# GpSimd multiplies rows and edges, and ScalarE takes half of the exponentials tile by tile, in the slots behind the last transfer of a graph-attention pass

## The reference, cut to what matters

```python
e = jax.nn.leaky_relu(feat_src[src] + feat_dst[dst]); e = jnp.sum(e * attn, axis=-1)
ee = jnp.exp(e - segment_max(e)[dst])
alpha = ee / segment_sum(ee)[dst]                 # one share per edge and head
msg = softmax(en * r_feat * alpha, axis=-1)       # en = feat_src[src], over the 32 features
g_agg = segment_sum(msg, dst)
```

## Time and profile before

| what | value |
|---|---|
| median of three runs | 5961.28 us |
| the profiled execution | 5973.71 us, span 5971.6 us |
| the tail from the end of the long loop to the final projection | about 5705 to 5914 us of the span |
| of it, steps after the last softmax piece | about 5758.7 to 5900.8 us |

### The profile page before, as it was taken

The page is one execution under the profiler, slowest core; times in us unless marked ns, Lnnn a source line. Parts: engine busy times, 40 slices in busy tenths (PEclk is TensorE's granted clock), DMA queues, the critical chain, the costliest instruction groups (busy, mean ns, idle before and its releaser), DMA issues. The chain is left out here.

```text
span 5971.6 us, 92359 instructions
## 1 busy us (share of the span) xinstructions
PE 4194.8 (70%) x31126; PEld 3201.6 (54%) x31126; DVE 2727.6 (46%) x6953; ACT 2238.6 (37%) x5687; POOL 3172.5 (53%) x3030
## 2 busy tenths in 40 slices
PE   4777777777867777778757577676666676666656
PEld 2444444444445555544557566566565665566646
DVE  6635444444211111234322355655556556466586
ACT  2555555555300000156200045445454454444520
POOL 4645545555145555553066566565555655565645
PEclk9898888888667777888555567676677766667776
DMA  2323343343257777400122223333333333333332
GB/s 83 144 99 141 141 155 150 149 155 147 91 208 256 255 251 257 153 9 7 46 53 51 59 70 85 79 85 85 76 84 79 79 89 74 80 86 81 85 84 64
DMA packets 324619, 660.29 MB, mean 111 GB/s; under 512 B 124556, under 2 KB 208454, under 8 KB 316232
## 3 DMA queue, kind: packets, MB, share of 16 engines
q1 hardware_dynamic: 230246, 581.33, 27.6%
q0 software_dynamic: 92160, 74.67, 7.7%
q10 hardware_dynamic: 1896, 0.12, 0.0%
HBM read 393.69 MB, written 262.14 MB: 110 GB/s over the span
## 5 line engine op out<-in xcount | busy, mean ns | idle before, releaser
L1667 POOL DMA_INDIRECT gath<-fs_scratch,src_idx x1568 | 1615.4, 1030 | 1158.1 <-issue 459.9
L681 POOL DMA_INDIRECT gath<-in_x,src_idx x720 | 767.4, 1066 | 724.9 <-PE sum_x_ps_g L791 442.1
L1716 PE MATMUL ps_e<-fdw,scratch 128*128 128x66 f32 x3136 | 789.7, 337 | 395.8 <-issue 195.1
L729 ACT ACTIVATE scratch<-sum_x_ps_c 128x800 bf16<-128x800 f32 x932 | 763.0, 836 | 669.6 <-PE sum_x_ps_c L748 469.0
L1796 ACT ACTIVATE scratch<-scratch,bias,weight 128x32 f32<-128x32 f32 x2608 | 931.2, 403 | 55.1 <-DVE bias L1869 47.8
L1718 PE MATMUL ps_e<-gath,ident 128*128 128x66 f32 x3136 | 785.8, 336 | 151.4 <-issue 150.7
L681 POOL DMA_INDIRECT gath<-y_scratch,src_idx x592 | 597.2, 1009 | 543.1 <-PE sum_y_ps_g L791 353.2
L1716 PEld LDWEIGHTS ps_e<-fdw,scratch 128*128 128x128 f32 x3136 | 639.6, 249 | 454.5 <-issue 419.2
L1779 ACT ACTIVATE scratch<-ps_o 128x512 f32<-128x512 f32 x394 | 227.9, 596 | 1446.9 <-remote 844.8
L748 PE MATMUL sum_x_ps_c<-e_tab,scratch 128*128 128x400 bf16 x1864 | 541.2, 378 | 320.1 <-ACT scratch L729 171.2
L1718 PEld LDWEIGHTS ps_e<-gath,ident 128*128 128x128 f32 x3136 | 648.3, 252 | 161.6 <-issue 161.4
(11 more groups left out here) (276 smaller groups left out, 5308.2 us busy)
## 6 DMA issues: line engine op xcount, KB each, us to landing
count_scratch<-scratch SPq DMA_DIRECT2D x60, 3200.0 KB
scratch<-count_scratch SPq DMA_DIRECT2D x240, 800.0 KB
en_scratch<-gath SPq DMA_DIRECT2D x196, 264.0 KB
scratch<-en_scratch SPq DMA_DIRECT2D x196, 264.0 KB
scratch<-in_edge_attr_2x SPq DMA_DIRECT2D x390, 128.0 KB
gath<-fs_scratch,src_idx POOLq DMA_INDIRECT x1568
fdw<-fd_scratch SPq DMA_DIRECT2D x392, 33.0 KB
gath<-in_x,src_idx POOLq DMA_INDIRECT x720
```

The costliest lines, as they stand in the source:

```text
L681: pool.indirect_dma_start(out=gath[:, s, t, 0:F], out_offset=None, in_=table_dram, in_offset=bass.IndirectOffsetOnAxis(ap=src_idx[:, g, k: ...
L729: act.activation(counts[:, b % 2, :, unit["column"]:unit["column"] + 2 * q] .rearrange("p a (h d) -> p h a d", h=2), ps_c[u % 2][:, :, 0:q ...
L1667: pool.indirect_dma_start(out=gath[:, s, t, :], out_offset=None, in_=fs_dram, in_offset=bass.IndirectOffsetOnAxis(ap=src_idx[:, g, k:k + 1 ...
L1716: pe.matmul(ps_e[g][:, k, 0:ROW], oht[:, s % 2, g * K + k, :], fdw[:, s, g, :], start=True, stop=False)
```

## The change

In the tail, the product of rows and edges moves from DVE to POOL. POOL makes it for slot n + 1 at the head of step n, ahead of its other work for slots n and n - 1; the product of the first tail slot is made before the tail begins. DVE waits for it (`tail_multiplied`) before it takes the maximum. The slot is then divided: tiles 0 to 3 go the way of the long loop (DVE copies the shares into `weight`, makes `bias` = - maximum x share, and ACT makes eight small exponentials with scale, bias and `accum_out`), tiles 4 to 7 the way of the tail before (POOL takes off the maximum and multiplies by the shares, ACT makes one exponential over the half). DVE sums only tiles 4 to 7. The long loop is unchanged.

```diff
+                def multiply(n, q):
+                    pool.wait_ge(loaded[q], arrived(n, q))
+                    feats = en[:, q, :, 0:HID]
+                    pool.tensor_tensor(feats, feats, r[:, q, :, :], ALU.mult).then_inc(tail_multiplied, 1)
 
                 def step(m, n, q, piece):
+                    if exists(n, -1):
+                        multiply(n + 1, (q + 1) % SLOTS)
                     if exists(n, 0):
                         pool.wait_ge(top_ready, n + 1)
-                        pool.tensor_tensor(heads(q), heads(q), each(bias[:, q, :]), ALU.subtract).then_inc(centred, 1)
+                        pool.tensor_tensor(later(q), later(q), of_later(bias[:, q, K * H:]), ALU.subtract)\
+                            .then_inc(centred, 1)
                         pool.wait_ge(centred, n - (TAIL - 1))
-                        pool.tensor_tensor(heads(q), heads(q),
-                                           each(a_tab[:, bass.ds(n * SG, SG), :, :].rearrange("p g k h -> p (g k h)")),
+                        pool.tensor_tensor(later(q), later(q),
+                                           of_later(a_tab[:, bass.ds(n * SG + 1, 1), :, :]
+                                                    .rearrange("p g k h -> p (g k h)")),
                                            ALU.mult).then_inc(scaled, 1)
...
+                multiply(TAIL, TAIL % SLOTS)
                 tail(pool, lambda it: None, step)
...
-                        if m is None:
-
-                            act.wait_ge(scaled, n - (TAIL - 1))
-                            act.activation(en[:, q, :, 0:HID], en[:, q, :, 0:HID], ACT.Exp).then_inc(exp_done, 1)
-                        else:
-                            act.wait_ge(bias_ready, n + 1)
-                        for i in range(ST * H if m is not None else 0):
+                        act.wait_ge(bias_ready, n + 1)
+                        for i in range(ST * H if m is not None else K * H):
...
+                        else:
+                            act.wait_ge(scaled, n - (TAIL - 1))
+                            act.activation(en[:, q, K:, 0:HID], en[:, q, K:, 0:HID], ACT.Exp).then_inc(exp_done, 1)
...
-                    if exists(n, 0):
+                    if exists(n, 0) and m is not None:
                         dve.wait_ge(loaded[q], arrived(n, q))
                         feats = en[:, q, :, 0:HID]
                         dve.tensor_tensor(feats, feats, r[:, q, :, :], ALU.mult).then_inc(multiplied, 1)
...
+                    if exists(n, 0) and m is None:
+                        shares = a_tab[:, bass.ds(n * SG, 1), :, :].rearrange("p g k h -> p (g k h)")
+                        dve.tensor_copy(weight[:, q, 0:K * H], shares)
+                        dve.wait_ge(top_ready, n + 1)
+                        dve.scalar_tensor_tensor(bias[:, q, 0:K * H], bias[:, q, 0:K * H], -1.0, shares,
+                                                 ALU.mult, ALU.mult).then_inc(bias_ready, 1)
...
-                        first = K if m is not None else 0
                         dve.wait_ge(exp_done, n)
-                        dve.tensor_reduce(total[:, q1, first * H:], en[:, q1, first:, 0:HID]
+                        dve.tensor_reduce(total[:, q1, K * H:], en[:, q1, K:, 0:HID]
```

More of the change, by code:

```diff
@@ L1523, in build, with arrived @@
                                 "msg_ready", "oh_msg_ready", "summed", "added"))
-            centred, scaled = sem("centred"), sem("scaled")
+            centred, scaled, tail_multiplied = sem("centred"), sem("scaled"), sem("tail_multiplied")
             block = ctx.enter_context(nc.Block())
             r_view = edge_attr.rearrange("e h f -> e (h f)")
+            def arrived(n, q):
+                if not isinstance(n, int):
+                    return slot_count(n, q, 16 * (1 + SG))
+                count = 0
+                for i in range(q, n + 1, SLOTS):
+                    count += 16
+                    for g in range(SG):
+                        count += 16 * (E - (i * SG + g) * GROUP >= K)
+                return count
             def walk(engine, before, step, lag=LAG):
@@ L1677, in each, with later, of_later @@
                     return wide(columns.rearrange("p (t h) -> p t h", h=H), 3, [P, ST, H, F])
+                def later(q):
+                    return en[:, q, K:, 0:HID].rearrange("p t (h f) -> p t h f", h=H)
+                def of_later(columns):
+                    return wide(columns.rearrange("p (t h) -> p t h", h=H), 3, [P, ST - K, H, F])
+                def multiply(n, q):
+                    pool.wait_ge(loaded[q], arrived(n, q))
+                    feats = en[:, q, :, 0:HID]
+                    pool.tensor_tensor(feats, feats, r[:, q, :, :], ALU.mult).then_inc(tail_multiplied, 1)
                 def step(m, n, q, piece):
+                    if exists(n, -1):
+                        multiply(n + 1, (q + 1) % SLOTS)
                     if exists(n, 0):
                         pool.wait_ge(top_ready, n + 1)
-                        pool.tensor_tensor(heads(q), heads(q), each(bias[:, q, :]), ALU.subtract).then_inc(centred, 1)
+                        pool.tensor_tensor(later(q), later(q), of_later(bias[:, q, K * H:]), ALU.subtract)\
+                            .then_inc(centred, 1)
                         pool.wait_ge(centred, n - (TAIL - 1))
-                        pool.tensor_tensor(heads(q), heads(q),
-                                           each(a_tab[:, bass.ds(n * SG, SG), :, :].rearrange("p g k h -> p (g k h)")),
+                        pool.tensor_tensor(later(q), later(q),
+                                           of_later(a_tab[:, bass.ds(n * SG + 1, 1), :, :]
+                                                    .rearrange("p g k h -> p (g k h)")),
                                            ALU.mult).then_inc(scaled, 1)
@@ L1859, in step @@
                     if exists(n, 0):
-                        dve.wait_ge(multiplied, n + 1)
+                        if m is not None:
+                            dve.wait_ge(multiplied, n + 1)
+                        else:
+                            dve.wait_ge(tail_multiplied, n - (TAIL - 1))
                         dve.tensor_reduce(top[:, :] if m is not None else bias[:, q, :],
@@ L1921, in step @@
                                           ALU.mult).then_inc(msg_ready, 1)
[L1923 to L1932, removed]
                 def row(n, lo=0, hi=P):
```

## The result

The changed kernel took 6000.82 us (median of 20 runs, 5951.84 to 6032.07) against 5964.05 us before (20 runs, 5915.14 to 6000.28): ratio 1.0056, 95% interval 1.0036 to 1.0077, so it is 21 to 46 us slower. The forecast was +25 us with T = 5.86 us a step, and "same" within 1%. The direction and the mechanism held; the size was on the low side. "Same" alone tells little: by the prediction's own sums it would have held for every T up to 7.05, so the tail has to tell the cases apart.

What follows compares the result with a forecast made beforehand. POOL with its port to DVE bounds the tail's step, the four-slot ring nearly tight; +27.8 us from a two-step round and -2.7 from softmax steps make +25, 5986 us, range 5946 to 6014.

Steps and rivals of the forecast that it cites:

- T: Time per message step in the tail's repeating part, 29 steps: 4.90 us before, forecast 5.86, adding 27.8 us.
- The round over two steps: Tail's slot ring, messages j to messages j + 2, closes over two steps instead of three: 11.46 us, 5.73 a step.
- The matmul term: PE's matmuls inside the round, taken as 2.80 us, the stretch's mean, between 3.67 at 1.2 GHz and 1.96 at 2.4.
- rival D: POOL's pause idles PE, matmuls run at 1.2 GHz: T 6.30, +38 us; with the ground towards it, chance 0.11.
- case A: The main forecast: two-step round with the one-hot in it, T 5.86, +25 us; chance 0.60.
- the 0.13 for irregular steps: Added to the tail's step because T before, 4.90, exceeded POOL's 4.77 by that much; kept unchanged in the forecast.
- The transfer: SP's transfers of the tail, from issue to product, inside the round: 3.87 us, read where DVE's product waited.
- The softmax steps: First four message steps, bound by DVE, which sheds 0.68 us a step: -2.7 us.
- What was costed at nothing: ACT's eight small exponentials plus one over half a slot, 3.7 us a step instead of 0.63, covered by ACT's idle time.
- C: Round does not close; POOL with its port sets the tail's step: T 4.60, -11 us, 5950; chance 0.13 with E.
- E: POOL's product would be ready long before the step, so nothing waits; same number as C; chance 0.13 with C.
- B: Same round without the one-hot in it, as DVE finds the port at another moment: T 5.37, +11 us, 5972; chance 0.16.

Runs made afterwards that it cites:

- e1: Changed kernel with the product of rows and edges put back on DVE, exponentials still split; T 4.71, tail 180.0 us, ratio to the kernel before 0.9993.
- e2: Kernel before with only the product moved to POOL, exponentials not split; T 6.42, tail 232.4 us, ratio to the kernel before 1.0084.
- e3: Changed kernel with POOL's product moved from the head of its step to behind the messages; T 5.86, tail 218.1 us, ratio to the kernel before 1.0058.
- e4: Changed kernel with DVE's one-hot at the head of steps without a softmax piece; T 5.77, tail 212.4 us, ratio to the kernel before 1.0063.
- e6: Changed kernel with the tail's edge transfers cut to one partition of 128, leaving out work; T 5.61, tail 205.6 us, no ratio.
- e10: Changed kernel with edge transfers issued once the product of slot n - 4 is done; T 5.62, tail 206.2 us, ratio to the kernel before 1.0033.
- e11: Changed kernel with 14 idle matmuls ahead of PE's wait in every even slot; T 5.72, tail 209.6 us, no ratio.
- e5: Changed kernel with 28 idle matmuls ahead of PE's wait in every even slot; T 5.97, tail 216.3 us, ratio to the kernel before 1.0058.
- e12: Kernel before, exponentials not split, with early reciprocals on DVE and early edge transfers on SP; T 4.71, tail 180.2 us, ratio to the kernel before 0.9994.
- e9: Changed kernel with product back on DVE, early reciprocals and early edge transfers; T 4.36, tail 169.9 us, ratio to the kernel before 0.9973.

## Why the prediction was right, and where its sizes were off

**The round over two steps** was right in kind. Moving the product put the wait for a transfer on an engine whose queue holds the messages; e1, e2 and e3 show it by taking the product away, alone, and behind, and e4, e6 and e10 by making single terms of the round smaller, each of which took the tail down with it. The pair summed to 11.46 in the prediction and to 12.99 in the pair shown above. Its terms: matmuls with the hand-over to SP 3.95, where I had 2.98; issue to product 4.33, where I had 3.87; product 1.14 for 1.05; halves 1.41 for 1.39; messages with the port 2.02 for 2.03.

**The matmul term was the mis-sized one.** I took the mean of the stretch, 2.80, for a duration that has two values and whose place decides which: the group in the round is the first after 6.0 to 7.7 us of idleness of PE, and in the pair shown it took about 3.8 us (5751.10 to SP's issue at 5755.05, less the hand-over); the one right behind it, outside the round, had the rest of the 5.91, about 2.1. It is not this pair alone: over the thirteen pairs the messages' end and SP's issue lie 3.7 to 4.1 us apart, 3.95 in the mean, where the sum had 3.12 (0.14 + 2.80 + 0.18). In e11, where PE had been kept busy, such a group took 1.96. The rival D had named this very mechanism with T = 6.30 and +38 us; the tail gave T = 6.21 and +37.1. What happened was case A's round with case D's clock, and I had given D and the ground towards it 0.11. That D's number came so near is partly luck: its round of 12.33 is short of the measured 12.65, the 0.13 for irregular steps stood in for the rest although the steps were regular, and the last of the 29 steps, which has no transfer to wait for and takes 3.87, pulls the mean of the others, 6.29, down to 6.21. The Trainium skill (SBUF — State Buffer, section Who interferes with whom) says that issue order decides who blocks, so the one-hot, having asked first, would go first; the trace agrees (messages 2.02 to 2.10 after each long wait) and e4 confirms its price, 6.21 to 5.77 in T.

**The transfer** counts from SP's first issue to POOL's product: 4.33 in the pair shown, 3.7 to 4.7 and 4.15 in the mean over the thirteen pairs, and not 3.87. I had read it where DVE waited. The row it came from stands at a turn of the tail's loop: in the kernel before, DVE's product starts after a pause of 0.73 or 0.74 us at five turns, and the view puts three of them (5779.35, 5838.89 and 5857.93) to a transfer and two (5799.88 and 5819.86) to nothing. So the 0.73 in the earlier trace rows need not be the transfer's, and 3.87 may be too long even there. Which part of the excess is a longer transfer and which is POOL's start after the release no run here separates.

**The softmax steps** were to give 2.7 us and gave 0.5 (41.42 for 41.96 from slot 162 to 165). DVE lost the product's 0.62 four times, but POOL's product came to stand against DVE's own instructions; one copy of 8 columns took 1.02 beside it instead of 0.16, and a scan 2.20 instead of the 1.35 at the same place before. e1, which leaves the product on DVE, needs 41.17 for these steps, so the product's move gained nothing here:

```profile
5677.32 1.18 POOL L1700 TENSOR_TENSOR scratch<-scratch 128x512 f32<-128x512 f32 x1 [5.48 <-DMA scratch<-in_edge_attr_2x]
5677.51 1.02 DVE L1896 COPY weight<-nodes 128x8 f32<-128x8 f32 x1
...
5688.73 2.20 DVE L1992 TENSOR_TENSOR_SCAN scratch<-scratch 128x512 f32<-128x512 f32 x1
```

**What was costed at nothing** held: ACT's 3.7 us a step (busy 104.3 of 180.2) was not what anyone waited for, and in e1, where T is lower, it still was not. (In e4, with the one-hot out of the way, DVE's sum did wait for ACT, 14 times, 12.5 us in all.) **Cases C and E** are out: POOL is idle for 69 of 180 us. **B** was out for the long steps, where the one-hot always took the port, and true of the short ones (messages 1.04).

With T = 6.21 for 5.86 over 29 steps (+10.2) and 2.2 less gained in the softmax steps, +25.1 becomes +37.5, against 37.1 in the tails and 21 to 46 in the times.

## What to carry to other kernels

Before moving a wait for a transfer to another engine, write down what is queued behind it there, and count over how many steps the ring of buffers then closes; one step fewer can cost more than any work moved. A ring's round must be summed with the durations at its own place, not with the stretch's means: the first matmul group after a long pause is the slow one. And where a change touches a thirtieth of a kernel, compare that stretch in the traces; the rest of the span moved by more, and in either direction, than the change did.

## What was not expected of the hardware

- A wait of one engine turned into alternating steps (8.5 and 4.5 us in the pair shown) rather than even ones of 6.2: two slots' transfers and matmul groups travel as a pair behind each other, and only the first of the pair is waited for.
- PE at work for 147.6 of 173.1 us in e5 had a granted clock of 0.99, at 98.2 of 169.9 us in e3 it had 0.60, and at 83.2 of 180.2 us in the changed kernel 0.73. Busy time alone does not order them: in e3 the groups come one by one with a pause of 2 to 3 us before each, in the changed kernel in pairs.
- A turn of the tail's loop costs DVE time of its own. In e12 three of four steps take 4.45 us and the fourth 5.39, and in that one DVE's product began after 0.86 us in which nothing in the profile held it. The pause comes at each of the loop's five turns, 0.86 to 0.88 us in e9 and e12 and 0.73 to 0.75 in e1; why it differs is open. Where the view names a transfer for such a pause, its length at the other turns tells whether the transfer is to blame:

```profile
5907.31 0.99 DVE L1887 TENSOR_TENSOR scratch<-scratch 128x512 f32<-128x512 f32 x1 [0.86 <-issue]
```
